# Last layer: the high half of g turned by DMA transposes instead of TensorE

## What is computed

```
X = rfftn(x, axes=(-2, -1)); Xr, Xi = real(X), imag(X)
Yr = conv3x3(Xr, wr) - conv3x3(Xi, wi) + b_real
Yi = conv3x3(Xr, wi) + conv3x3(Xi, wr) + b_imag
out = x + irfftn(complex(Yr, Yi))
```

## Time and profile before

| | |
|---|---|
| median of 3 runs | 5166.97 us (5162.87 to 5169.14) |
| the profiled execution, its own time | 5166.33 us |
| its span in the trace | 5164.4 us |
| last layer, from its first load to the end | 4005.6 to 5164.4 us |
| PE busy over the span | 94% |
| DVE / ACT / POOL busy over the span | 72% / 66% / 29% |
| granted TensorE clock | 0.989 of full speed |

### The profile page before, as it was taken

How to read it: one execution, slowest core, us unless ns; L and a number is a source line. 1 busy time by engine, 2 the same in 40 slices (tenths; PEclk the granted TensorE clock), 3 DMA queues, 4 the chain that set the end, 5 groups by cost and what they waited for, 6 DMA issues and landing times. The chain is left out here.

```text
span 5164.4 us, 176760 instructions
## 1 busy us (share of the span) xinstructions
PE 4871.3 (94%) x76605; PEld 2923.4 (57%) x76605; DVE 3723.3 (72%) x6707; ACT 3384.5 (66%) x3511; POOL 1510.5 (29%) x1801
## 2 busy tenths in 40 slices
PE   4999999999999999999999979997777899999998
PEld 2444544444447967568875533444555566666665
DVE  4653553553534888888888868887999688888888
ACT  1222222231224888888888878885998798989897
POOL 1102102102102221222222100003776355555556
PEclk9999999999999999999999989999999999999999
DMA  8778778778757877878787769996886466666664
GB/s 259 232 247 267 234 247 267 238 246 258 236 191 204 242 222 229 237 223 238 233 226 241 223 221 325 323 324 238 308 309 261 111 151 152 150 154 149 154 149 119
DMA packets 368016, 1167.24 MB, mean 226 GB/s; under 512 B 75689, under 2 KB 76328, under 8 KB 297386
## 3 DMA queue, kind: packets, MB, share of 16 engines
q1 hardware_dynamic: 342040, 1131.78, 72.2%
q0 software_dynamic: 23040, 21.76, 1.5%
q10 hardware_dynamic: 2162, 2.39, 0.2%
HBM read 683.58 MB, written 453.51 MB: 220 GB/s over the span
## 5 line engine op out<-in xcount | busy, mean ns | idle before, releaser
L734 PE MATMUL c_p<-c_w,wc 128*32 128x512 f16 x27648 | 1518.7, 380 | 25.3 <-DMA c_w<-xs 19.9
L812 ACT ACTIVATE c_t<-c_p,cbias,cscale 128x512 f32<-128x512 f32 x512 | 397.9, 777 | 1273.7 <-PE c_p L734 1273.7
L734 PEld LDWEIGHTS c_p<-c_w,wc 128*32 128x32 f16 x27648 | 753.1, 96 | 762.3 <-issue 26.6
L734 PE MATMUL c_p<-c_w,w 128*32 128x512 f16 x19456 | 1145.0, 379 | 3.5 <-issue 3.4
L734 PEld LDWEIGHTS c_p<-c_w,w 128*32 128x32 f16 x19456 | 758.5, 96 | 316.3 <-issue 7.1
L639 DVE TENSOR_SCALAR c_y<-c_t 128x512 f16<-128x512 f32 x256 | 111.8, 437 | 644.7 <-ACT c_t L812 593.6
L1818 PE MATMUL f_P<-f_qh,f_wt 64*64 64x512 f16 x4608 | 545.7, 378 | 1.8 <-DVE f_t L1714 1.8
L1818 PE MATMUL f_P<-f_hl,f_wt 64*64 64x512 f16 x4608 | 545.3, 379 | 0.0
L817 ACT ACTIVATE c<-c_w 64x2052 f16<-64x2052 f16 x256 | 492.5, 1924 | 11.9 <-DMA c_w<-ys 5.7
L818 ACT ACTIVATE c<-c_w 64x2052 f16<-64x2052 f16 x256 | 492.9, 1925 | 6.2
L1979 POOL TENSOR_TENSOR f_y<-f_y,f_x 128x512 f32<-128x512 f32 x256 | 330.8, 1292 | 449.2 <-DVE f_hl L1693 443.1
(11 more groups left out here) (275 smaller groups left out, 7826.3 us busy)
## 6 DMA issues: line engine op xcount, KB each, us to landing
c_w<-xs SPq DMA_DIRECT2D x576, 264.0 KB, 8.2
d_x<-x SPq DMA_DIRECT2D x128, 1024.0 KB, 7.6
x<-d_x SPq DMA_DIRECT2D x128, 1024.0 KB, 5.1
c_w<-ys SPq DMA_DIRECT2D x144, 528.0 KB
xs<-a_hl SPq DMA_DIRECT2D x70, 1056.0 KB, 11.1
a_x<-in_x SPq DMA_DIRECT2D x256, 256.0 KB, 5.7
a_x<-in_x SPq DMA_DIRECT2D x128, 512.0 KB, 4.8
x<-a_x SPq DMA_DIRECT2D x512, 128.0 KB, 6.1
```

The source lines that it names most:

```text
L734: t = p.matmul(pg[32 * j:32 * j + 32, :], weights[:, var], source[:, j, at:at + NW], start=start, stop=stop, tile_position=(0, 32 * j))
L812: s.activation(tt_[n % 3][:, :], pp[:, n % 4, :], ACT.Tanh, bias=cbias[:, blk:blk + 1], scale=cscale[:, blk:blk + 1]).then_inc(c_act, 1)
```

## The change

The high half of g is no longer turned by TensorE. SyncE issues DMA transposes from `hl` straight to `gT`: for a row item two of them, 64 rows by 512 columns of float16 each (the two swap the halves of the rows), for each of the first four items one of 48 rows. TensorE's `turn` keeps the four transposes of the low half, ScalarE's `turn` copies half of what it did, and `tp` is half as wide. `gT` has three tiles (NT) in place of two. TensorE's `hilbert` waits in addition for the transposes' semaphore `f_td`. In SyncE's step z the new `turn(z+1)` stands first, ahead of `store(i-3)` and `load(z+8)`; it waits for `f_hi` of item z+1 and for `hilbert(z-2)`.

```
-    NXF, LAG = 20, 6
+    NXF, LAG, NT = 20, 6, 3
...
-        gT = [sb(ctx, f"f_gT{i}", [128, 2, 2, 2, 128], F16) for i in range(2)]
+        gT = [sb(ctx, f"f_gT{i}", [128, 2, 2, 2, 128], F16) for i in range(NT)]
...
-        tp = ps(ctx, "f_tp", [128, 1024], F16)
+        tp = ps(ctx, "f_tp", [128, 512], F16)
...
+        f_td = [sem(f"f_td{i}") for i in range(NT)]
...
+        def n_turned(i):
+
+            return sum(16 if r < NB else 32 for r in range(i % NT, i + 1, NT))
...
-                    for z in range(8):
-                        l, pi, kx = z // 4, z // 2 % 2, z % 2
-                        t = p.transpose(tv[:, z, 0:n], h[0:n, l, pi, 128 * kx:128 * kx + 128], id16[0:n, 0:n])
+                    for z in range(4):
+                        pi, kx = z // 2, z % 2
+                        t = p.transpose(tv[:, z, 0:n], h[0:n, 1, pi, 128 * kx:128 * kx + 128], id16[0:n, 0:n])
                     t.then_inc(f_tp, 1)
 
                 def hilbert(i, a_):
-                    n, T = item(i)[2], gT[i % 2]
+                    n, T = item(i)[2], gT[i % NT]
                     if a_ == 0:
+                        p.wait_ge(f_td[i % NT], n_turned(i))
                         p.wait_ge(f_gt, i + 1)
...
-                    Tv = gT[i % 2][:, :, :, :, :].rearrange("p l a k n -> p (l a k) n")
+                    Tv = gT[i % NT][:, 1].rearrange("p a k n -> p (a k) n")
                     s.wait_ge(f_tp, i + 1)
-                    if i >= 2:
-                        s.wait_ge(f_qp, i - 1)
+                    if i >= NT:
+                        s.wait_ge(f_qp, i - NT + 1)
...
+                def turn(i):
+                    n, h, T = item(i)[2], place(i)[0], gT[i % NT][:, 0].rearrange("p a k n -> p (a k) n")
+                    e.wait_ge(f_hi, i + 1)
+                    if i >= NT:
+                        e.wait_ge(f_qp, i - NT + 1)
+                    for first, to, rows in ((64, 0, 64), (0, 64, 64)) if i >= NB else ((0, 0, n),):
+                        e.dma_start_transpose(T[:, :, to:to + rows], h[first:first + rows, 0].rearrange("p a w -> p (a w)")).then_inc(f_td[i % NT], 16)
+
                 for i in range(NB, 12):
                     load(i)
                 load_w(0)
                 load_w(1)
+                turn(0)
                 for z in range(NI + LAG + 3):
                     i = z - LAG
+                    if z + 1 < NI:
+                        turn(z + 1)
                     if 0 <= i - 3 < NI:
                         store(i - 3)
```

## The result

The changed kernel takes 5237.27 us (median of 4 runs, 5225.43 to 5242.77) where the kernel before took 5164.92 (4 runs): ratio 1.0137, interval 1.0117 to 1.0156. It is slower by 72 us or 1.4%, where the forecast was 5115 us and faster. The profiled execution has a span of 5233.6 us.

A forecast was written before the change was run, and what follows sets the result against it. PE was taken to bound the last layer at 4.28 us per item, falling to 4.05. The sum was 5166.3 - 56 (PE) + 5 (start) = 5115 us; range 5095 to 5310, the likeliest case's own 5099 to 5127.

The forecast's parts named there:

- What bounded the kernel: Last layer's steady stretch: PE always busy, 4.28 us per item; no wait or other engine breaks the pattern.
- PE's term: Four of eight transposes leave PE: 0.23 us less per item, 245 items, 56 us (49 to 67).
- SyncE's queue: SyncE's issuing per item: 1.33 us now, 3.83 with two transposes, fitting PE's 4.05 with 0.22 to spare.
- h: Time one DMA transpose's issue holds SyncE's sequencer: taken as 1.2 us, ends 0.59 and 2.6.
- The first rival: SyncE's queue becomes the bound from h = 1.42 on; slower, 5257 us at h = 1.6; chance 0.25.
- the prediction's last part: Signs of right (PE full, item 4.05 us) or wrong (PE's `hilbert` idles for `f_gT`, SyncE never idle).
- Landing: Transposed half of `gT` arriving for `hilbert`: second transpose 3.1 to 8.1 us including issue delay, covered, at the top barely.
- the cover of 8.5 us: Time from the end of `high(z+2)` to `hilbert(z+2)` in PE's step z+3, available for the transposes to land.
- This rival: Turned half lands late, deciding above a landing of 8.5 us; 10 us gives 5237 us; chance 0.02.
- DMA engines: Engines 61% busy, 2.61 us per item; two transposes add 0.53, making 3.1 of 4.05 us: fits.
- The rival of transposes one after the other: In the DMA engines each transpose starts only when the one before landed; 5298 us at 2.4 each; chance 0.08.
- Start: First items' turns wait behind SyncE's early loads and delay tile moves: 5 us, bounds 0 and 10.

## Why the prediction was wrong

*What bounded the kernel, and PE's term:* right. Four transposes less are worth 0.220 us per item (0.23 said), 53 us with no DMA in their place. ACT's copy fell to 0.594 us and neither ACT, DVE nor POOL became the bound.

*SyncE's queue:* this is the step that failed, and it was the one called weakest. It said that SyncE "needs 1.43 + 2h" and "I double the copy and take h = 1.2", so 3.83 us, "it fits, with 0.22 us to spare". The median is 1.24, so the guess of the ordinary issue was good, but its reason was not: 256-byte pieces leave a copy at 0.62, and 16 packets leave a transpose at 1.21. What was mis-sized is the mean, 1.42 us, since the sum goes by means: 0.43 us more per item. The other terms grew too. Store, load and weights hold 1.40 us per item where they held 1.26 (0.60 + 0.50 + 0.64/4), and the gaps between five issues are 0.27 where about 0.17 was counted. 3.83 + 0.43 + 0.14 + 0.10 = 4.50. The rows warned of it: the load's longest of 1623 ns beside a median of 457, the copy's 2614 beside 589. They were read as ends of a range, not as a tail that a full queue has to carry. "The loads of this layer average barely over their 0.46" (0.50) did not hold for transposes.

*The first rival*, SyncE as the bound, is what happened: with PE waiting for the transposes, issue rows and no idle SyncE, as the prediction's last part listed. Its threshold of h = 1.42 was put on the mean that came out; by its own sum that is a draw, and the growth of the other terms made it slower. The chance of 0.25 was too small for a margin of 0.22 us in 4.05.

*Landing:* 2.5 to 7.2 us from the issue, median 4.7, where 1.9 to 6.9 was taken from copies. With the loads off the queue it is most of what is left of the loss, up to 9.5 us; the cover of 8.5 us was said to be enough and is not. This rival had 0.02.

*DMA engines:* the share forecast, 3.1 of 4.05 us or 0.77, is what copies of the same bytes show (0.73 and 0.77); transposes show 0.94, of which 0.19 is the few packets of over 200 ns. The rival of transposes one after the other is not shown: the two landings of an item lie within 0.3 us of each other in 37 of the 59 pairs on record, as 4508.31 and 4508.61 us for the pair issued from 4503.54 on. The figure of the Trainium skill (VectorE: DVE Perf Modes, The three transpose paths), 1309 ns for a 128x128 block by DMA, is near the hold of 1.24 us, but here that is the price of an issue of 64x512 as of 16x512; it can't be multiplied by blocks.

*Start:* 5 us said, 0 to 10 as bounds, 16 measured. The named cause is right and worth 12 us, as measured with copies; it was put at 4. That it grew because all the first items' turns pass one after the other behind the early loads is argued, not shown.

## What to carry to other kernels

Before work is moved to the queue of an engine that only issues DMAs, add up how long each issue holds it, by the mean and not the median, with 0.05 to 0.1 us of gap for each, and compare with the period: its idle time is a resource like that of any engine, and a margin of a few per cent is none, since issues of 1 to 3 us come up that only idle time absorbs. DMA transposes are bought by the instruction: here 1.21 to 1.24 us at the median, whether 16 or 64 rows, so few and large ones. One transpose of all 128 rows per item, with the swap of the halves put elsewhere, would halve the issues; no measured run shows it (kernels of this form, and one that turns both halves by DMA, gave no time), nor how long an issue of 128 rows holds. Moving store and weights off the queue as well was not tried.

## What was unexpected of the hardware

The hold of a transpose does not depend on its size from 16 to 64 rows of 512 columns (1.21 to 1.24 us), nor on its packets (16 of 1 KB or 256 of 256 bytes), and is twice that of a copy inside SBUF (0.53 to 0.62). A DMA share of 0.94 at only 173 GB/s, where 256-byte copies moved 192 GB/s at 0.77, did not set the time, and a fifth of it lay in the 2.5% of the small packets that took over 200 ns. And moving the loads to another engine's queue did not help the transposes land sooner: 4.8 us at the median, with the longest on record grown from 7.2 to 9.5.
